# Values of all four batches at the head of the last stage, contexts 2 and 3 loaded as the expert slots fall free

## The reference

```python
x = x + tanh(g_xattn[0]) * L0_xattn(layernorm(x), ctx)
x = x + tanh(g_ffn[0])   * (shared(xn) + expert[argmax(xn @ Wg)](xn))
kp, vp = ctx @ Wk.T, ctx @ Wv.T + bv          # 512 context rows of one batch
qp = layernorm(x) @ Wq.T + bq
x = x + tanh(g_xattn[1]) * (softmax(qp @ kp.T / 16) @ vp @ Wo.T + bo)
x = x + tanh(g_ffn[1])   * (butterfly(gelu(butterfly(layernorm(x) @ We + be) + ub)) @ Wc + ...)
```

## Time and profile before

| | us |
|---|---|
| median of 3 runs | 772.37 (772.19 to 772.91) |
| the profiled execution | 773.89 |
| its span, first to last instruction | 772.1 |
| TensorE busy | 704.7 |
| VectorE busy | 615.7 |
| ScalarE busy | 367.1 |
| GpSimd busy | 418.5 |

### The profile page before, as it was taken

How to read it: one execution, slowest core, us unless ns; L and a number is a source line. 1 busy time by engine, 2 the same in 40 slices (tenths; PEclk the granted TensorE clock), 3 DMA queues, 4 the chain that set the end, 5 groups by cost and what they waited for, 6 DMA issues and landing times.

```text
span 772.1 us, 12693 instructions
## 1 busy us (share of the span) xinstructions
PE 704.7 (91%) x4375; PEld 589.1 (76%) x4375; DVE 615.7 (80%) x957; ACT 367.1 (48%) x634; POOL 418.5 (54%) x304
## 2 busy tenths in 40 slices
PE   5659999999999989889999999999986899999996
PEld 3438888777888878657777777777775899989996
DVE  5688999999999964889987777777787767687653
ACT  1313333334343421356777666666633665555643
POOL 4777888888888881414986666676023101110000
PEclk8868999999999999999999999999999999999999
DMA  9300000000127012141454416100010101000000
GB/s 290 159 19 23 23 21 22 20 20 27 34 41 336 8 62 69 35 170 35 171 194 181 171 60 242 28 28 22 14 35 20 36 28 55 28 28 8 16 14 20
DMA packets 24289, 54.32 MB, mean 70 GB/s; under 512 B 3152, under 2 KB 20304, under 8 KB 23088
## 3 DMA queue, kind: packets, MB, share of 16 engines
q1 hardware_dynamic: 19056, 45.54, 16.4%
q0 software_dynamic: 1872, 5.11, 2.4%
...
...
## 4 chain that ended last, share of the span: by engine, by line
PE 42%; DVE 12%; issue 5%; ACT 5%; DMA 1%; POOL 0%; DVEq 0%; ACTq 0%; POOLq 0%
PE bank L729 17%; PE bank L720 13%; PE bank L979 8%; PE bank L737 3%; DVE SLOT_r L1891 2%; DVE PRODV_r L1891 2%; DVE STC L1979 1%; ACT L1425 1%; ACT XS L1425 1%; DVE NM L2029 1%; ACT SLOT_r L1429 1%; DVE X L2050 1%; ACT SLOT_r L1399 1%; DVE X L2001 1%; DVE SLOT L2047 1%
## 5 line engine op out<-in xcount | busy, mean ns | idle before, releaser
L608 POOL TENSOR_TENSOR PRODV<-SHARED 128x2048 f32<-128x2048 f32 x32 | 144.5, 4516 | 31.4 <-DVE bank L1597 27.9
L720 PEld LDWEIGHTS bank<-ROWS,SLOT 128*128 128x128 f32 x1024 | 121.0, 194 | 1.6
L720 PE MATMUL bank<-ROWS,SLOT 128*128 128x128 f32 x1024 | 121.3, 278 | 0.0
L699 POOL TENSOR_TENSOR RS<-VE,MHALF 128x2 f32<-128x2 f32 x16 | 13.1, 818 | 150.4 <-DVE VE L1986 150.4
L720 PE MATMUL bank<-SLOT,XST 128*128 (+1 forms) x184 | 83.9, 599 | 0.5 <-ACT XST L1323 0.5
L1519 DVE TENSOR_TENSOR PRODQ<-bank,SHARED 128x4096 f32<-128x4096 f32 x16 | 70.7, 4418 | 10.6 <-PE bank L720 5.9
L610 POOL TENSOR_TENSOR PRODV<-PRODV 128x1024 f32<-128x1024 f32 x32 | 74.7, 2333 | 2.5
L1528 DVE TENSOR_REDUCE bank<-PRODQ 128x256 f32<-128x4096 f32 x16 | 70.7, 4419 | 0.1
L623 POOL DMA_INDIRECT XS<-normal_rows,INV x23 | 28.4, 1236 | 72.0 <-PE bank L737 50.7
L1891 DVE TENSOR_TENSOR PRODQ_r<-SLOT,ROWS_r 128x1024 fp32r<-128x1024 f32 x44 | 63.8, 1450 | 0.5 <-ACT ROWS_r L1333 0.5
L720 PE MATMUL bank<-SLOT,HA 128*128 128x256 f32 x256 | 59.2, 384 | 2.4 <-DVE HA L1715 2.0
...
## 6 DMA issues: line engine op xcount, KB each, us to landing
...
X<-x SPq DMA_DIRECT2D x16, 128.0 KB, 2.2
SHARED<-ctxT SPq DMA_DIRECT2D x16, 128.0 KB, 2.3
normal_rows<-ROWS SPq DMA_DIRECT2D x16, 128.0 KB, 1.7
WET<-ctxT SPq DMA_DIRECT2D x4, 512.0 KB, 7.9
out<-X SPq DMA_DIRECT2D x16, 128.0 KB, 1.7
expert_rows<-YS ACTq DMA_DIRECT2D x12, 128.0 KB, 1.7
expert_rows<-PICK ACTq DMA_DIRECT2D x11, 128.0 KB, 1.7
```

The source lines that it names most:

```text
L608: gp.tensor_tensor(o, pr, v, ALU.mult).then_inc(s["av_prod"], 1)
L720: last = pe.matmul(dst, lhs(k), rhs(k), start=(k == 0), stop=(k == chunks - 1))
```

## The change

Values of all four batches are made early: those of batch 2 ahead of unit 0, those of batch 3 within unit 0. All four contexts, their high and low parts, and all four V1 and V1L get buffers of their own. Contexts 2 and 3 lie in the upper half of PRODV (`flatV`), which the last expert tile reads, so SP loads them when `slot_uses` reaches NT + 1. Their high parts lie in ROWS, those of 0 and 1 in W0.

- ScalarE makes the high parts of contexts 0 and 1 in the last step of stage B, around the first four `turned_fold`, and those of 2 and 3 between the values ahead of unit 0.
- VectorE drops the cast and subtraction for context 0, the cast for context 1 and the two bias sums. GpSimd makes the bias sums and the low part of context 0 (`late_sums`), and values(0,0) waits for it.
- fold(0) goes behind values(1,1); values(2,0) and (2,1) go before flips(0); values(3,0) goes between scores(1) and attend(0), values(3,1) between flips(1) and attend(1). Units 3 and 5 lose their values, units 2 and 4 their context splits.
- SP issues all context loads before it waits for the first output.

```diff
+        CTXB = [v[:, r * KD * L:(r + 1) * KD * L].rearrange("p (k t) -> p k t", k=KD)
+                for v in (WET[:, :, :].rearrange("p c d -> p (c d)"), flatV[:, KF * D:2 * KF * D]) for r in range(2)]
...
-        V1 = [part(TB * D).rearrange("p (t d) -> p t d", t=TB) for _ in range(2)]
+        V1 = [part(TB * D).rearrange("p (t d) -> p t d", t=TB) for _ in range(B)]
...
+        V1L += [part(TB * D).rearrange("p (t d) -> p t d", t=TB) for _ in range(2)]
+        CTXH = [v[:, r * KD * L:(r + 1) * KD * L].rearrange("p (k t) -> p k t", k=KD)
+                for v in (W0, ROWS) for r in range(2)]
...
-            uses = [("values", 0, 0), ("values", 0, 1), ("fold", 0), ("values", 1, 0), ("values", 1, 1), ("fold", 1),
-                    ("queries", 0), ("fold", 2), ("fold", 3)]
+            uses = [("values", 0, 0), ("values", 0, 1), ("values", 1, 0), ("values", 1, 1), ("fold", 0),
+                    ("values", 2, 0), ("values", 2, 1), ("fold", 1), ("queries", 0), ("fold", 2), ("fold", 3),
+                    ("values", 3, 0), ("values", 3, 1)]
...
             def load_ctx(b):
                 if b >= 2:
-                    sp.wait_ge(c["sc_done"], TB * (b - 1))
-                sp.dma_start(CTXB[b % 2], ctxT[:, b * L:(b + 1) * L].rearrange("(k p) t -> p k t", p=P))\
+                    sp.wait_ge(slot_uses, NT + 1)
+                    sp.wait_ge(c["ctx_high"], b - 1)
+                sp.dma_start(CTXB[b], ctxT[:, b * L:(b + 1) * L].rearrange("(k p) t -> p k t", p=P))\
...
+            gp.tensor_tensor(BCD[:, :], BIAS[:, 2, :], BIAS[:, 3, :], ALU.add).then_inc(late_sums, 1)
+            gp.wait_ge(pair_sb, 4)
+            gp.tensor_tensor(BVO, BVO, BIAS[:, 1, :], ALU.add).then_inc(late_sums, 1)
+            low, high_part = [v[0].rearrange("p k t -> p (k t)") for v in (CTXB, CTXH)]
+            gp.wait_ge(c["ctx_high"], 1)
+            gp.tensor_tensor(f32r(low), low, rounded(high_part), ALU.subtract).then_inc(late_sums, 1)
...
             def values(b, r):
-                pe.wait_ge(ctx_split, b + 1)
+                if b == 0:
+                    pe.wait_ge(late_sums, 3)
+                else:
+                    pe.wait_ge(ctx_split, b)
...
                 if has_up:
                     up(u - 1, 0)
+                else:
+                    values(3, 0)
                 attend(2 * u)
...
                     up(u - 1, 3)
+                else:
+                    values(3, 1)
                 attend(2 * u + 1)
-                if has_values:
-                    for r in range(2):
-                        values((u + 1) // 2, r)
...
+            for r in range(2):
+                values(1, r)
             fold(0)
             for r in range(2):
-                values(1, r)
+                values(2, r)
             flips(PB[0], 0, 0, "c_xn", "c_xT")
...
                 elif t2 is not None:
                     turned_hidden(t2, 0)
                     turned_hidden(t2, 1)
+                    act.wait_ge(slot_uses, NT)
+                    context(0)
                     for n in range(4):
                         turned_fold(n)
+                    context(1)
...
             values(0, 0)
             values(0, 1)
+            act.wait_ge(slot_uses, NT + 1)
+            context(2)
+            for r in range(2):
+                values(1, r)
+            context(3)
             fold(0)
             for r in range(2):
-                values(1, r)
+                values(2, r)
             copies(PB[0], 0, "c_xT", XN3T, "c_xT_hi")
...
             for n in range(4):
                 lower_turned_fold(n)
-            dve.wait_ge(slot_uses, NT)
-            split_context(0)
-            dve.tensor_tensor(BCD[:, :], BIAS[:, 2, :], BIAS[:, 3, :], ALU.add).then_inc(bcd_ready, 1)
-            dve.tensor_tensor(BVO, BVO, BIAS[:, 1, :], ALU.add).then_inc(bcd_ready, 1)
+            lower_context(1)
             for n in range(4, KF):
                 lower_turned_fold(n)
-            dve.wait_ge(slot_uses, NT + 1)
-            split_context(1)
...
                 if has_up:
                     lower_hidden(u - 1, 0)
+                else:
+                    lower_values(3, 0)
                 attended(2 * u)
...
+                if not has_up:
+                    lower_values(3, 1)
                 if has_next:
                     lower_queries(u + 1)
...
-            dve.wait_ge(bcd_ready, 2)
+            dve.wait_ge(late_sums, 3)
             lower_values(0, 0)
             lower_values(0, 1)
-            lower_fold(0)
+            lower_context(2)
+            lower_values(1, 0)
             next_rows(0)
             next_stats(0)
-            lower_values(1, 0)
+            lower_values(1, 1)
             norm_rows(0, 0, "c_rstd", "c_xT", "c_xn")
-            lower_values(1, 1)
+            lower_fold(0)
             lower_rows(PB[0], 0, "c_xT_hi", XN3T, XN3TL, "c_xT_sb")
+            lower_values(2, 0)
+            lower_values(2, 1)
+            lower_context(3)
             lower_fold(1)
             next_rows(1)
             next_stats(1)
```

77 lines of the change are left out of this document (27 added, 50 removed).

## The result

The changed kernel takes 779.42 us (median of 4 runs, 777.40 to 780.07), the kernel before 772.64 us in the same session (772.19 to 773.12). The ratio is 1.0077, 95% interval 1.0062 to 1.0093: slower by 0.8%, where 773.1 us had been forecast, in a range that ended at 775.4. The profiled execution took 777.40 us, with a span of 775.6 us, against 773.89 and 772.1: it shows 3.5 us of the difference.

What follows compares the result with a forecast made beforehand. TensorE's list bounds the late units; at the stage's start TensorE mostly waits for VectorE. Start +2.9, unit 0 +1.65, clock +0.8, late saving -4.7 give +0.65 on 772.4: 773.1 us, range 770.6 to 775.4.

Steps and rivals of the forecast that it cites:

- the expert rows: Start of last stage: write 1.7 us slower beside the loads, 0.5 given back; next_rows(0) at 571.4 instead of 570.20.
- the clock: At scores(0), after an idle 2.9 us: a likely fall of the granted clock to 0.50, taken as 0.8 us.
- Late saving: Units 3 and 5 without their values become as short as their neighbours: 4.7 us less, 0.4 kept for the range.
- doesn't save late: Rival: the long units were long for another reason, at most half of 4.7 us comes back; 775.4 us, chance 0.04.
- Before the first values: End of stage B: GpSimd's subtraction of 2.33 us ends at 563.0, before values(0,0) at 563.73; costs nothing.
- The loads do not hold up ScalarE: Start of last stage: context 2 lands at 567.6, ScalarE's copy starts by 567.7, and the load costs nothing.
- The rival that ended on the slower side: Loads hold up ScalarE at context(2), landing at 570 instead of 567.6: +1.9 us more, 775.0 us, chance 0.28.
- VectorE's list: From the turned rows to scores(0): 6.5 us of VectorE work, so scores(0) starts at 583.4, 2.9 us later.
- Unit 0: values(3,0) and values(3,1) and their low parts, put into the gaps of unit 0, cost 1.65 us together.
- The 0.5 us given back: Second gather instruction, formerly 1.61 us beside context 1's cast and subtraction: 0.5 us credited because that work moved.
- rival on ScalarE: Context(2) lands late in ScalarE's list ahead of values and fold(0): +1.9 us more, 775.0 us, chance 0.28.
- a gather at 572: Start of last stage: later expert rows, counted in the forecast's upper end within the 0.32 for slower by over 0.2%.

Runs made afterwards that it cites:

- e5: The changed kernel run again with no edit; 776.27 us, ratio 1.0054 to the kernel before.
- e3: The changed kernel with VectorE's low part of context 2 moved behind next_stats(0); 777.2 us in one run.
- e8: The changed kernel with VectorE's low part of values(1,1) ahead of next_rows(0) and that of context 2 behind next_stats(0); 779.4 us, ratio 1.0073.
- e6: The changed kernel with 12 idle matmuls between values(2,0) and values(2,1); 776.39 us, ratio 1.0043 to the kernel before.
- e1: The changed kernel with context 2 loaded during stage B and context 3 after the first gathers, its splits later; 771.9 us, ratio 0.9968 to the kernel before.
- e4: The changed kernel with VectorE's low part of values(1,1) moved ahead of next_rows(0); 775.3 us, ratio 1.0023 to the kernel before.
- e11: e1 with VectorE's list reordered and 6 and 8 idle matmuls ahead of the scores of units 0 and 1; 770.45 us, ratio 0.9964.

## Why the prediction was wrong

Its structure held nearly everywhere; two terms of the sum were too small, the one for the expert rows (+1.2 us) and the one for the clock (+0.8).

**Right.** *Late saving*: forecast 4.7 us, with 0.4 kept for the context splits; measured 135.0 - 129.8 = 5.1. The rival "doesn't save late" is refuted by the intervals of 21.8 us. *Before the first values*: GpSimd's subtraction took 2.42 us, forecast 2.33, and values(0,0) started at 563.25, not late. *The loads do not hold up ScalarE*: they landed 3.8 us after their issue, and the copy of context 2 started at 566.87, by 567.7 as forecast. The rival that ended on the slower side named the wrong place. *VectorE's list*: from the turned rows (581.21) to scores(0) (587.73) 6.52 us; forecast 6.5, and 6.52 in e5 as well (576.48 to 583.00). *Unit 0*: from `lower_queries(0)` to the row maximum of unit 1 the profile has 23.29 us against 21.83, +1.46; forecast 1.65.

**Too small: the expert rows.** `next_rows(0)` was to start at 571.4, 1.2 us later; it started at 573.89, and since the copy of the last expert rows ran 0.36 us earlier that is 4.05 us more. Of these 2.03 are the write (3.74 against 1.71, forecast 1.7). The 0.5 us given back for the second gather's instruction did not come: 1.55 us against 1.61, as the low part of context 2 took the place of that of context 1 beside it. The sum's own list of VectorE has it there. Had it come, the rows would have been earlier by 0.3 to 0.6 us, as `next_rows(0)` in e3 and the fifteenth mark in e8 show. The other 2.0 are the gather's landing, 5.42 us after its issue against 3.43 (570.20 - 566.77), which in e5 was 3.2; there the whole term is 1.9 us, not 4.05. So the step that failed first is +1.2 = 1.7 - 0.5: it was 1.9 us at least, 0.3 too little for the write, because "the overlap here is less complete", and 0.5 given back for nothing. On top came, in the profiled execution, 2.0 us of a late gather, for which the sum had no term; that this can happen was not to be seen in the rows, and that it did in the first profile is chance.

**Too small, and in the wrong place: the clock.** The sum had 0.8 us for scores(0). In the profile the fall comes earlier, over values(2,1) and the flips: from the start of values(2,1) to the turned rows it took 581.21 - 576.79 = 4.42 us, forecast 576.9 - 574.1 = 2.8; scores(0) ran at 1.00. Ahead of it stands the gap before values(2,1), expected at 2 us and measured at 5.22, of which 4.1 is VectorE's wait for the expert rows. With that gap filled (e6) or shorter (1.05 us in e1) no fall came there, so the two errors are probably one chain: the late rows make the gap, and the gap the low clock. In e5, with rows 2 us earlier and a gap of 3.07, values(2,1) took 2.28 us and scores(0) 2.40 instead of 1.67.

**The sum again**, by the profile and against +0.65 forecast: expert rows +2.85 beyond the forecast, values(2,1) to turned rows +1.6, `next_rows(0)` to values(2,1) 2.90 instead of 2.7, +0.2, clock at scores(0) -0.8, unit 0 -0.2, late -0.4, start of the stage -0.36. Together +3.5, as measured. By the profile of e5, counted from the copy of the last expert rows: expert rows +0.7 beyond the forecast, `next_rows(0)` to values(2,1) +0.2, values(2,1) to turned rows +1.0, scores(0) to the row maximum of unit 1, clock included, +1.1 (24.45 us against 20.90, forecast 2.45 more), late -0.45. Together +3.2 with the 0.65; measured 3.1 (212.2 - 209.1). In both profiles these two terms are the bulk of the miss. The medians are apart by 6.8 us and, in e5, by 3.3: the profiled execution of the changed kernel was the fastest of its four, and that of the kernel before lay above its median. The offset of 1.5 us that the prediction carried over unchanged was a property of one execution, not of the kernel. How many stretches at 1.2 GHz an execution has differs from one to the next (mean granted clock 0.969 to 0.977 in the four runs, 0.966 to 0.980 in e5's six). A mean lower by 0.01 is 0.01 x 776 / 0.5 = 15.5 us more at the lower level. How much of the rest of the difference between the medians this explains isn't shown run by run.

The list of what would prove the prediction wrong named neither: a gather disturbed more than assumed stood only inside the rival on ScalarE ("a gather 0.9 us later than I take it"), and as "a gather at 572" in the upper end of the forecast. Its own row, 2.2 us more for a write beside two loads, lay nearer to what was measured here (2.0 to 2.1 more) than the 1.7 after the discount.

## What to carry to other kernels

When a transfer is moved next to a small one on which the critical path hangs, take the measured price of such an overlap in full, even if the overlap looks partial. What counted here was how much of the large transfer stood ahead of the small one: half the bytes didn't halve the price (3.7 us with 1 MB, 3.6 with 512 KB, 2.4 with 128 KB, 1.7 alone). Then load into a buffer that is free earlier, or let the critical transfer go first and check who waits for the load next. Where TensorE's work is moved to the start of a stage that waits for another engine, follow that engine's list for the instruction that frees the next bank, and put it ahead of the instruction that waits for a DMA.

## What the runs showed beyond that

- A write of 128 KB alone landed in 1.7 us; beside loads issued some 0.4 us earlier by another engine it took 2.4, 3.6 and 3.7 us (128 KB, 512 KB, 1 MB). Its first packet started 0.8 us after the issue alone, 1.0 with 128 KB, and 2.3 us after it with 512 KB and with 1 MB.
- The instruction of an indirect gather on GpSimd took 0.95 us with VectorE at other work, and 1.47 to 1.68 us beside a VectorE subtraction of 128 x 1024 with both operands in SBUF. Fifteen of the sixteen 4-byte packets of the gather had ended 1.3 to 1.5 us after the end of the instruction in 15 of 16 profiles, so the arrival followed the instruction.
- The sixteenth came 1.2 us or more after the fifteenth in two profiles (changed, e8). In both, one 16 KB packet of the queue "instruction" (0.96 and 0.97 us) had run in between.
- The same kernel with the same lists had its low clock once over values(2,1) and the flips (6.8 us in one piece) and once in three pieces of 3.4 us with 10.2 us in all. A gap of 5.22 us had the first after it; one of 2.25 us ahead of the flips in e4 had none, where in the kernel before one of 2.31 us had the earlier trace rows.
- The best version (e11: no load beside the write, lists reordered, gaps ahead of scores filled) ran at 0.9964 [0.9952, 0.9976] of the kernel before; e1 alone at 0.9968 [0.9958, 0.9979].
